# A two-layer network on one core: the second layer's tiles set between the last steps of the first layer

## The chip, the cores and the metric

The kernel runs on one core of a Trainium2 chip. The metric is device time in microseconds (us) for one execution, lower is better; the median of three runs is given.

## The reference

The input is x of 8 batches of 512 tokens of width 256, and a condition of 64 numbers for each batch. Everything is float32 at the interface. Two layers follow one another.

```
layer 0:  h  = gamma * x * rsqrt(mean(x*x) + eps) + beta            (gamma, beta from the condition)
          x  = x + alpha * W_o(softmax(q k^T / 4) v)                (16 heads of 16)
          h  = the same norm with its own gamma and beta
          x2 = x + alpha' * (out_w(silu(gate_w h) * (hidden_w h)) + out_b)      (1024 hidden)
layer 1:  h  = x2 * scale * rsqrt(mean(x2*x2) + eps)                (scale from the condition)
          val, gate = up_w h                                        (1024 each)
          h  = val * gelu(gate)                                     (exact gelu)
          y  = quantised(h, 127 levels a token) @ ternary(down_w)^T
          out = y + x2
```

## The kernel before

**First layer.** `STEPS` is 32. A batch takes up to three times 32 steps, and three batches are in work at once: iteration i prepares batch i+1 (norm, projections), runs the scores and weights of batch i, and does the output projection and the feed-forward part of batch i-1. Iterations go from -1 to 8. Every engine has its own instruction stream, written out by the same walk over iterations and steps z (`run_pipeline`, `timeline`); a step's time T says in which iteration and step it falls (T modulo 32 is z). Engines meet only by semaphores; `need` writes such a wait. Each engine takes its stream strictly in order.

For the last batch (number 7) the scores' row maxima (`maxima`, L693) run to iteration 7, z=17, the scores, exponentials and weighted sums to z=28 and 30; `heads_out` (L708) is at z=0 of iteration 8, `turn_o` at z=1, `project_o` at z=4 and 5, the residual, squares, `xnorm`, turning (`norm_t`), `affine`, and the split into a high part on ScalarE and a low part on GpSimd by z=11. The feed-forward part has 16 chunks (`T_GH`, z=14 to 28, two of them in z=19): `gate_hidden` makes 12 products into bank gen[n % 2], ScalarE takes the tanh, VectorE two operations (`swiglu`, L740), ScalarE and GpSimd split the result (`a_high`, `a_low`), and `swiglu_down` makes 6 products two steps later. Two chunks are under way at once. Products are made in three passes of high and low parts (`exact`, L895). In iteration 8 all of this has no other batch beside it.

**Ternary weights.** In iteration 8, z=4, VectorE sums the absolute values of down_w, scales, rounds (L758 to L773), with a small product and 16 turnings on TensorE; the raw weights are loaded once the last scores are made, into the space of the stacked queries and keys (qst, kst), and the result goes where the values were (vst).

**Second layer.** Only when both halves of x2 of the last batch are made, TensorE turns the 32 blocks of up_w (`transpose_weights`, eight groups of four; ScalarE and VectorE split them), into the space of the gate weights. Then 32 tiles of 128 tokens, in a software pipeline of its own (`iteration_b`, a step a tile). In step k: VectorE `scale_b` of tile k+1 (L829), `norm_b` of k+2, `h_mul(0)` of k, `finish` of k-2, `h_mul(1)`, `q_copy` (L859) of k-1, `quantise` (L842 to L854) of k; TensorE `unit(0)` of k (12 products with 512 columns), `down` of k-2 (L1152), `unit(1)` of k, `q_transpose` of k-1 (L1145), `norm_t_b` of k+2; ScalarE the high part of h for k+1 (L625), square of k+3 (L629), gelu for both halves (L634); GpSimd the root, the low part and the rounding (`integers`). The turned x2 has its bank in gen[0] (`xt_bank`), the down product in gen[1] (`down_bank`).

Names and lines that come up: DVE = VectorE, ACT = ScalarE, POOL = GpSimd, SP = the queue that issues DMAs. L693 row maxima, L895 all three-pass products, L974 weighted sums, L1010 turn_o, L722/L727 low parts of o, L738 residual, L669 xnorm, L679 affine, L743/L747 swiglu, L552 a_high, L661 low parts of turned weights, L761 to L773 ternary weights.

## Time and profile before

| | us |
|---|---|
| median of 3 runs | 1233.23 |
| lowest, highest | 1226.01, 1234.82 |
| the profiled execution, its own time | 1228.62 |
| its span, first to last instruction | 1226.8 |

Times in the trace count from the start of the span. The span and the time lie 1.8 us apart, so a difference in the one is a difference in the other. TensorE's clock is shown as the share of full speed that was granted, between two levels, 1.2 and 2.4 GHz.

### The profile page before, as it was taken

The page shows a single profiled execution, that of the slowest core. Times are in us where ns is not written, and L with a number is a line of the kernel's source. Part 1 is how long each engine was busy: PE and PEld are TensorE (multiplying, and loading weights), DVE is VectorE, ACT ScalarE, POOL GpSimd, SP SyncE. Part 2 cuts the span into 40 slices and gives each one's busy share as a digit, 9 for nine tenths or more (in the row PEclk, how much of TensorE's full clock was granted, in tenths as well). Part 3 has the DMA queues.
Part 4 walks back from the last instruction along what each step waited for, and adds up shares of the span by engine and source line. Part 5 has one row for each costly group of instructions (what it writes and reads, how often), then busy time and mean ns, then how long its engine had stood idle before and what let it go on. Part 6 is the DMA issues. An engine that isn't in the chain of part 4 may idle for free.

```text
span 1226.8 us, 19035 instructions
## 1 busy us (share of the span) xinstructions
PE 1077.7 (88%) x6775; PEld 739.2 (60%) x6775; DVE 812.8 (66%) x1613; ACT 557.8 (45%) x1242; POOL 300.3 (24%) x372
## 2 busy tenths in 40 slices
PE   6467787998989899899989989988976989999997
PEld 4312324675577467557646746753856867777775
DVE  4165556667756866775786677676443468888886
ACT  3215445655645654574566557455532332322321
POOL 0401101321321232132123213211213233333331
PEclk8757878999999999999999999998987889999999
DMA  5362624606152360634426065250040011121111
GB/s 171 77 114 51 138 49 88 128 30 135 58 100 38 98 141 17 135 75 83 64 98 131 5 132 100 58 118 2 2 150 1 28 38 53 53 63 54 53 59 36
DMA packets 87758, 92.69 MB, mean 76 GB/s; under 512 B 10241, under 2 KB 85001, under 8 KB 86641
## 3 DMA queue, kind: packets, MB, share of 16 engines
q1 hardware_dynamic: 87664, 91.49, 33.3%
q8 instruction: 54, 0.88, 0.3%
q14 instruction: 40, 0.32, 0.1%
HBM read 61.68 MB, written 29.78 MB: 75 GB/s over the span
## 4 chain that ended last, share of the span: by engine, by line
PE 71%; DVE 10%; DMA 6%; issue 4%; SPq 3%; POOL 3%; ACT 3%; POOLq 0%; DVEq 0%; ACTq 0%
PE gen L895 27%; PE core L895 13%; PE pvb L974 9%; PE core L948 7%; PE core L962 7%; DVE negmax L693 4%; DMA xa<-in_x_dram 3%; SPq L310 2%; PE gen L1152 2%; ACT xn L522 1%; DVE xn L669 1%; PE gen L935 1%; POOL stat L430 1%; PE pvb L1145 1%; DMA v_d<-v 1%
## 5 line engine op out<-in xcount | busy, mean ns | idle before, releaser
L693 DVE TENSOR_REDUCE negmax<-core 128x1 f32<-128x512 f32 x512 | 338.6, 685 | 216.8 <-PE core L948 214.6
L534 ACT ACTIVATE p<-core 128x512 f32<-128x512 f32 x512 | 278.2, 597 | 189.7 <-PE core L962 187.3
L948 PE MATMUL core<-kst,qst 96*128 96x512 bf16 x512 | 202.5, 413 | 60.4 <-DVE negmax L693 26.5
L895 PE MATMUL gen<-hs,wgh 128*128 128x256 f32 x1536 | 221.2, 295 | 9.1 <-DVE a L747 5.8
L895 PEld LDWEIGHTS gen<-hs,wgh 128*128 128x128 f32 x1536 | 198.4, 192 | 28.0 <-DVE a L747 9.0
L895 PE MATMUL core<-wgh,hs 128*128 128x512 f32 x768 | 193.8, 402 | 1.8 <-POOL hs L490 1.8
L450 POOL TENSOR_TENSOR a<-a 128x256 fp32r<-128x256 f32 x128 | 93.6, 731 | 333.0 <-ACT a L552 333.0
L962 PE MATMUL core<-qst,kst 99*128 99x512 bf16 x512 | 163.8, 400 | 8.0 <-ACT p L534 4.9
L895 PEld LDWEIGHTS core<-wgh,hs 128*128 128x128 f32 x768 | 140.8, 190 | 30.5 <-POOL hs L490 2.4
L948 PEld LDWEIGHTS core<-kst,qst 96*128 96x128 bf16 x512 | 47.1, 99 | 184.6 <-DVE negmax L693 80.5
L974 PE MATMUL pvb<-p,vst 128*32 128x512 f32 x1024 | 129.0, 623 | 0.0
L895 PE MATMUL gen<-wout,a 128*128 128x256 f32 x768 | 113.0, 285 | 1.1 <-POOL a L450 1.1
L552 ACT CAST a<-a 128x256 fp32r<-128x256 f32 x128 | 52.0, 406 | 111.9 <-DVE a L747 86.1
L895 PEld LDWEIGHTS gen<-wout,a 128*128 128x128 f32 x768 | 100.2, 190 | 3.5 <-ACT a L552 1.3
L625 ACT CAST hs<-h 128x256 fp32r<-128x256 f32 x32 | 13.0, 407 | 155.4 <-DVE h L834 155.4
L743 DVE SCALAR_TENSOR_TENSOR ug<-th,gen 128x256 f32<-128x256 f32 x128 | 52.8, 412 | 39.6 <-ACT th L547 39.6
L962 PEld LDWEIGHTS core<-qst,kst 99*128 99x128 bf16 x512 | 51.2, 102 | 46.0 <-ACT p L534 14.1
L840 DVE TENSOR_TENSOR qst<-core,p 128x512 f32<-128x512 f32 x64 | 44.2, 692 | 40.2 <-PE core L895 22.9
L974 PEld LDWEIGHTS pvb<-p,vst 128*32 128x32 f32 x1024 | 27.5, 112 | 70.2 <-issue 66.8
L496 POOL TENSOR_SCALAR kst<-qst 128x1024 bf16<-128x1024 f32 x32 | 33.4, 1044 | 143.4 <-DVE qst L854 143.4
L547 ACT ACTIVATE th<-gen 128x256 f32<-128x256 f32 x128 | 48.8, 381 | 42.0 <-PE gen L895 39.3
L428 POOL TENSOR_SCALAR stat<-stat 128x4 f32<-128x4 f32 x16 | 3.1, 193 | 257.9 <-ACT xn L522 257.9
(137 smaller groups left out, 1284.2 us busy)
## 6 DMA issues: line engine op xcount, KB each, us to landing
parts_d<-qk SPq DMA_DIRECT2D x32, 384.0 KB, 2.6
qst<-parts_d SPq DMA_DIRECT2D x96, 128.0 KB, 4.7
kst<-parts_d SPq DMA_DIRECT2D x96, 128.0 KB, 7.8
v_d<-v SPq DMA_DIRECT2D x8, 1024.0 KB, 11.2
vst<-v_d SPq DMA_DIRECT2D x16, 512.0 KB, 6.0
xa<-in_x_dram SPq DMA_DIRECT2D x8, 512.0 KB, 9.4
xr<-in_x_dram SPq DMA_DIRECT2D x8, 512.0 KB, 8.8
x_d<-x SPq DMA_DIRECT2D x8, 512.0 KB, 7.3
```

The costliest lines, as they stand in the source:

```text
L450: pool.tensor_tensor(a2[1][:, n % 2, :], a32[:, n % 2, :], a2[0][:, n % 2, :].bitcast(F32), ALU.subtract).then_inc(s["a_lo"], 1)
L496: pool.tensor_scalar(qi[t % 2], q32[t % 2], -ROUND, 1.0, ALU.add, ALU.mult).then_inc(s["qi_"], 1)
L534: act.activation(p32[:, ring(b, m), k * S:(k + 1) * S], stb[k], ACT.Exp, scale=SCALE).then_inc(s["exp_"], 1)
L547: act.activation(th[:, n % 2, :], gen[n % 2][:, 0:HALF], ACT.Tanh, scale=0.5).then_inc(s["tanh_"], 1)
L552: act.copy(a2[0][:, n % 2, :], a32[:, n % 2, :]).then_inc(s["ah"], 1)
L693: dve.tensor_reduce(negmax[:, n // TT, n % TT:n % TT + 1], smb[n % 2], AX_X, ALU.max, negate=True).then_inc(s["smax"], 1)
L743: dve.scalar_tensor_tensor(out=ug[:, n % 2, :], in0=th[:, n % 2, :], scalar=1.0, in1=gen[n % 2][:, 0:HALF], op0=ALU.add, op1=ALU.mult).the ...
L840: dve.tensor_tensor(hb[t % 2][:, c * S:(c + 1) * S], stb[c], ge[:, c, 0:S], ALU.mult).then_inc(s["hmul"], 1)
L895: last = pe.matmul(out_, l, r, start=start and i == 0, stop=stop and i == len(passes) - 1, **kw)
L948: pe.matmul(smb[n % 2], qst[0:KROWS, h, q * P:(q + 1) * P], kst[0:KROWS, h, :], start=True, stop=True).then_inc(s["smax_mm"], 1)
L962: last = pe.matmul(stb[k], kst[0:KROWS + NPART, h, kt * P:(kt + 1) * P], qst[0:KROWS + NPART, h, :], start=True, stop=True)
L974: last = pe.matmul(pvb[j * VW:(j + 1) * VW, :], vst[:, kt, GROUP * g + j, :], p32[:, ring(b, m - 1 + j // 2), (j % 2) * S:(j % 2 + 1) * S] ...
```

## The change

The tiles of the second layer are written into the same walk as the steps of the first. From iteration 7, z=30 on (`Z_TILES`), every step holds half of a tile's step: even ones `first_half` (scale_b, norm_b, unit(0), h_mul(0), down, finish, the squares and the low part), odd ones `second_half` (unit(1), q_transpose, norm_t_b, h_mul(1), q_copy, quantise, integers). So `unit` of tile 0 is at z=4 and 5 of iteration 8, and that of tile 13 at z=30 and 31; tiles 14 to 31 follow in `run_after`. Further:

- The ternary weights are made at z=10 to 13 of iteration 7, one part a step, with their two turnings of eight blocks in bank gen[1].
- The up weights are turned at z=29, 30, 31 of iteration 7 and z=0 of iteration 8, two groups a step, in the four banks of the scores.
- For the last batch all chunks use bank gen[0] (so gate_hidden n waits for the swiglu of n-1), and chunk operations of VectorE, ScalarE and GpSimd stand in the same step as the products, after the other work and ahead of the half tile. o and its projection use gen[0] and gen[2].
- gen[1] is both the bank of the turned x2 and, in its other half, that of the down product. `down` waits in addition until the tile three further on is scaled, `norm_t_b` until the tile four before is finished.
- Buffers move so that nothing of the last batch is overwritten.

```diff
-    Z_TERN = 4
+    Z_TERN = 10
+    Z_UP = 29
+    Z_TILES = 30
+    T_SLOTS = 2
...
-        wup = wgh
+        wdown = sb("wdown", [P, KF, D], BF16)
...
+        wup = [nc.alloc_sbuf_tensor_at(f"wup{n}", [P, KD, 2 * F], F32R, offset=stack_at + n * H * S * 2) for n in range(2)]
...
+        raw_up = [v3_flat.rearrange("p (n i) -> p n i", i=D), raw_hp[:, :].rearrange("p (n i) -> p n i", i=D)]
+        raw_down = v3_flat[:, 0:KD * F]
...
-        xt_bank = gen[0][:, 0:KD * P]
-        down_bank = gen[1][:, 0:D]
+        xt_bank = gen[1][:, 0:KD * P]
+        down_bank = gen[1][:, D:2 * D]
...
+        up_bank = smb + stb
+        tern_bank = gen[1][:, :].bitcast(BF16)
+        def two_banks(b, pair):
+            return (0, 2) if b == B - 1 else pair
+        def gh_bank(b, n):
+            return gen[0] if b == B - 1 else gen[n % 2]
...
+        FIRST_TILE = L_SQ3
+        N_BETWEEN = STEPS - Z_TILES + STEPS
+        def run_between(i, z, first_half, second_half):
+            n = z - Z_TILES if i == B - 1 else z + STEPS - Z_TILES if i == B else -1
+            if n >= 0:
+                (first_half, second_half)[n % T_SLOTS](tile_at(FIRST_TILE + n // T_SLOTS))
+        def run_after(first_half, second_half):
+            for step in range(FIRST_TILE + N_BETWEEN // T_SLOTS, B * TT + L_DOWN):
+                first_half(tile_at(step))
+                second_half(tile_at(step))
...
# SP
+                if i == B - 1:
+                    sp.wait_ge(s["v_st"], 16 * B)
+                    sp.dma_start(raw_down.rearrange("p (r i) -> p r i", i=F), w["down_w"].rearrange("(r p) i -> p r i", p=P)).then_inc(s["raw_down_load"], 16)
...
+                if i == B - 1:
+                    sp.wait_ge(s["tern_t_"], 2)
+                    for n in range(2):
+                        sp.dma_start(raw_up[n], w["up_w"][n * F:(n + 1) * F, :].rearrange("(r p) i -> p r i", p=P)).then_inc(s["raw_up_load"], 16)
+                for z in range(STEPS):
+                    run_between(i, z, first_half, second_half)
...
# ScalarE
+                    for n, t in enumerate(T_GH):
+                        for b in at(z, t):
+                            if b == B - 1:
+                                tanh(b, n)
+                                a_high(b, n)
+                    for n in range(len(WG_UP) // 2):
+                        if i * STEPS + z == (B - 1) * STEPS + Z_UP + n:
+                            split_up(n)
+                    run_between(i, z, first_half, second_half)
...
# VectorE
+                    if i == B - 1 and 0 <= z - Z_TERN < 4:
+                        ternary_weights(z - Z_TERN)
+                    for n, t in enumerate(T_GH):
+                        for b in at(z, t):
+                            if b == B - 1:
+                                swiglu(b, n)
...
+            def first_half(at):
+                for b, t in at(L_H3):
+                    scale_b(b, t)
+                for b, t in at(L_XN3):
+                    norm_b(b, t)
+                for b, t in at(0):
+                    h_mul(b, t, 0)
+                for b, t in at(L_DOWN):
+                    finish(b, t)
+            def second_half(at):
+                for b, t in at(0):
+                    h_mul(b, t, 1)
+                for b, t in at(L_QT):
+                    q_copy(b, t)
+                for b, t in at(0):
+                    quantise(b, t)
...
# TensorE
-                need(pe, "a_", NCH, b, n - 1)
+                need(pe, "a_", NCH, b, n if b == B - 1 else n - 1)
...
+            def ternary_weights(step):
+                if step == 0:
+                    pe.wait_ge(s["xt_"], 2 * (B - 1))
+                    pe.wait_ge(s["wsum"], 1)
+                    pe.matmul(gen[1][:, 0:1], ones[:, :], wabs[:, :], start=True, stop=True).then_inc(s["wsum_mm"], 1)
+                if step >= 2:
+                    n = step - 2
+                    pe.wait_ge(s["tern"], 1)
+                    if n == 1:
+                        pe.wait_ge(s["tern_c"], 1)
...
+                need(pe, "final", TT, b, t - L_DOWN + L_XT3 + 1)
...
                 need(pe, "q_tc", TT, b, t + 1)
                 need(pe, "final", TT, b, t)
+                pe.wait_ge(s["h32_3"], KD * min(b * TT + t + L_DOWN - L_H3 + 1, B * TT))
                 for j in range(KF):
                     last = pe.matmul(down_bank, qT[t % 2][:, j * P:(j + 1) * P], wdown[:, j, :], start=(j == 0), stop=(j == KF - 1))
...
+            run_pipeline(pe, iteration)
+            run_after(first_half, second_half)
```

## Rows read from the trace of the kernel before

**Rows 1.** The page: busy time of each engine; the chain that ended last.
```profile
PE 1077.7 (88%) x6775; PEld 739.2 (60%) x6775; DVE 812.8 (66%) x1613; ACT 557.8 (45%) x1242; POOL 300.3 (24%) x372
...
PE 71%; DVE 10%; DMA 6%; issue 4%; SPq 3%; POOL 3%; ACT 3%; POOLq 0%; DVEq 0%; ACTq 0%
```
**Rows 2.** Windows: PE, PEld, DVE, ACT, POOL busy; clock; DMA share; GB/s.
```profile
902.30:937.30 35.00, 16.27 (x109) 13.19 (x107) 17.35 (x27) 6.70 (x18) 5.17 (x6) 0.71 0.38 132
937.30:974.70 37.40, 35.97 (x288) 35.28 (x288) 14.76 (x34) 12.15 (x32) 14.09 (x17) 0.95 0.00 1
974.70:989.00 14.30, 7.78 (x38) 6.82 (x37) 9.45 (x18) 7.02 (x18) 3.10 (x7) 0.64 0.36 110
989.00:1215.50 226.50, 226.19 (x1308) 179.34 (x1308) 183.06 (x375) 59.79 (x151) 75.77 (x120) 0.99 0.17 51
1215.50:1226.80 11.30, 4.33 (x33) 2.67 (x32) 5.17 (x10) 0.00 (x0) 1.04 (x1) 0.75 0.08 28
```
**Rows 3.** Timeline of one steady tile: start, duration, engine, line, operation.
```profile
1038.04 0.62 PE L1145 MATMUL pvb<-ident_bf,kst 128*128 128x128 bf16 x8
1038.30 0.69 DVE L840 TENSOR_TENSOR qst<-core,p 128x512 f32<-128x512 f32 x1 [0.44 <-PE core L895]
...
1041.26 0.75 DVE L854 TENSOR_SCALAR qst<-qst,qs 128x1024 f32<-128x1024 f32 x1
...
1041.49 1.05 PE L1152 MATMUL gen<-vst,kst 128*128 128x256 bf16 x8
1041.92 0.60 DVE L834 TENSOR_SCALAR h<-gen,cur 128x128 f32<-128x128 f32 x2
...
1045.14 0.62 PE L1145 MATMUL pvb<-ident_bf,kst 128*128 128x128 bf16 x8
```
**Rows 4.** Timeline of the ternary weights, VectorE.
```profile
913.50 2.28 DVE L761 TENSOR_REDUCE wabs<-kst 128x1 f32<-128x2048 f32 x1
...
919.43 1.23 DVE L771 TENSOR_SCALAR kst<-kst 128x2048 bf16<-128x2048 f32 x1
...
922.64 1.22 DVE L773 COPY vst<-core 128x2048 bf16<-128x2048 bf16 x1 [1.98 <-PE core L1058]
```
**Rows 5.** Timeline in iteration 7, about z=11: VectorE's row maxima.
```profile
849.74 3.10 DVE L693 TENSOR_REDUCE negmax<-core 128x1 f32<-128x512 f32 x5
```
**Rows 6.** Timeline of the last batch's own chain and of the turned weights.
```profile
910.32 1.91 PE L1010 MATMUL gen<-ident,o 128*128 128x128 f32 x8 [1.68 <-DVE o L717]
...
912.09 1.49 DVE L727 TENSOR_TENSOR hs<-gen,hs 128x512 fp32r<-128x512 f32 x2 [1.82 <-ACT hs L572]
...
925.65 0.69 DVE L738 TENSOR_TENSOR x<-th,xr 128x512 f32<-128x512 f32 x1
...
930.83 1.14 DVE L669 TENSOR_SCALAR xn<-x,stat 128x256 f32<-128x256 f32 x4 [3.07 <-POOL stat L430]
...
933.25 1.59 DVE L679 TENSOR_SCALAR h<-gen,cur 128x512 f32<-128x512 f32 x2 [1.28 <-PE gen L935]
...
978.86 0.69 DVE L661 TENSOR_TENSOR wgh<-gen,wgh 128x512 fp32r<-128x512 f32 x1 [0.16 <-ACT wgh L516]
```
**Rows 7.** The chain that ended last, in order of time: a chunk; the squares.
```profile
876.57 2.13 PE gen L895 x18
...
927.71 1.71 ACT xn L522 x8
```
**Rows 8.** Timeline of a chunk of the last batch: tanh, first swiglu operation, cast.
```profile
966.94 0.38 ACT L547 ACTIVATE th<-gen 128x256 f32<-128x256 f32 x1 [0.35 <-PE gen L895]
...
967.36 0.42 DVE L743 SCALAR_TENSOR_TENSOR ug<-th,gen 128x256 f32<-128x256 f32 x1 [1.21 <-ACT th L547]
...
968.26 0.41 ACT L552 CAST a<-a 128x256 fp32r<-128x256 f32 x1 [0.94 <-DVE a L747]
```
**Rows 9.** Groups by line, ScalarE, 1020 to 1200 us: gelu.
```profile
L634 ACT ACTIVATE p<-core 128x512 f32<-128x512 f32 x51 | 30.0, 588 | 2.5
```
**Rows 10.** Timeline: ScalarE ahead of the first gelu.
```profile
989.01 1.28 ACT L634 ACT_TABLE_LOAD   x1
```

More of the change, by code:

```diff
@@ L546, in tanh @@
                 need(act, "u_", NCH, b, n - 1)
-                act.activation(th[:, n % 2, :], gen[n % 2][:, 0:HALF], ACT.Tanh, scale=0.5).then_inc(s["tanh_"], 1)
+                act.activation(th[:, n % 2, :], gh_bank(b, n)[:, 0:HALF], ACT.Tanh, scale=0.5).then_inc(s["tanh_"], 1)
             def a_high(b, n):
@@ L571, in o_high @@
                     need(act, "o_t", KD, b, k + 1)
[L572 removed]
+                    act.copy(hs[0][:, k, :], gen[two_banks(b, OT_BANK)[k]][:, :]).then_inc(s["oh"], 1)
             def iteration(i, *there):
@@ new lines, in iteration, with split_up, first_half @@
+                    run_between(i, z, first_half, second_half)
+            def split_up(n):
+                for g in (2 * n, 2 * n + 1):
+                    act.wait_ge(s["up_t"], g + 1)
+                    act.copy(WG_UP[g][1][0], up_bank[g % 4]).then_inc(s["up_hi"], 1)
+            def first_half(at):
+                for b, t in at(L_HH3):
+                    if b == 0 and t == 0:
+                        act.wait_ge(s["up_t"], len(WG_UP))
+                    need(act, "h32_3", KD * TT, b, KD * (t + 1))
+                    need(act, "v2_mm", 2 * TT, b, 2 * (t + 1 - TT))
+                    a = slice(t * P, (t + 1) * P)
+                    act.copy(hp[0][:, :, a], h32_b[:, :, a]).then_inc(s["hh3"], 1)
+                for b, t in at(L_SQ3):
+                    if b == 0 and t == 0:
+                        act.wait_ge(s["pv_mm"], NG * KT * B)
+                    need(act, f"x2_ld{t}", 16, b, 16)
+                    need(act, "xt3", TT, b, t + 1 - TT)
+                    act.activation(xn_b[:, t, :], xa[:, t, :], ACT.Square, accum_out=stat[:, 1, 0, t:t + 1]).then_inc(s["sq3"], 1)
+                for b, t in at(0):
+                    gelu(b, t, 0)
@@ L639, in _, with second_half, gelu @@
+            def second_half(at):
+                for b, t in at(0):
+                    gelu(b, t, 1)
+            def gelu(b, t, c):
+                need(act, "g_mm", 2 * TT, b, 2 * t + c + 1)
+                need(act, "hmul", 2 * TT, b, 2 * t + c - 1)
+                act.activation(ge[:, c, :], smb[c], ACT.Gelu).then_inc(s["gelu"], 1)
+            run_pipeline(act, iteration)
+            run_after(first_half, second_half)
         @block.vector
@@ L816, in iteration @@
                             qk_rest(b, j)
-            run_pipeline(dve, iteration)
-            split_lo(WG_UP, "up_hi", "up_lo")
+                    if i == B - 1 and 0 <= z - Z_TERN < 4:
+                        ternary_weights(z - Z_TERN)
+                    for n, t in enumerate(T_GH):
+                        for b in at(z, t):
+                            if b == B - 1:
+                                swiglu(b, n)
+                    for n in range(len(WG_UP) // 2):
+                        if i * STEPS + z == (B - 1) * STEPS + Z_UP + n:
+                            split_up(n)
+                    run_between(i, z, first_half, second_half)
             def norm_b(b, t):
@@ L1115, in iteration @@
                             turn_group(b, m // (2 * KT))
-            run_pipeline(pe, iteration)
-            pe.wait_ge(s["x2_"], 2 * B)
-            pe.wait_ge(s["raw_up_load"], 16)
-            transpose_weights(WG_UP, "up_t", "up_lo")
-            pe.wait_ge(s["up_lo"], len(WG_UP))
-            pe.wait_ge(s["tern_c"], 1)
+                    if i == B - 1 and 0 <= z - Z_TERN < 4:
+                        ternary_weights(z - Z_TERN)
+                    for n in range(len(WG_UP) // 2):
+                        if i * STEPS + z == (B - 1) * STEPS + Z_UP + n:
+                            turn_up(n)
+                    run_between(i, z, first_half, second_half)
             def norm_t_b(b, t):
@@ L1138, in unit @@
                     need(pe, free, 2 * TT, b, 2 * t + c - 1)
-                    exact(bank, [(col(hs, k, t * P, P), col(wup, k, first + c * S, S)) for k in range(KD)]).then_inc(s[sem_], 1)
+                    exact(bank, [(col(hp, k, t * P, P), col(wup, k, first + c * S, S)) for k in range(KD)]).then_inc(s[sem_], 1)
             def q_transpose(b, t):
+                if b == 0 and t == 0:
+                    pe.wait_ge(s["o_norm"], NG * B)
                 need(pe, "qi_", TT, b, t + 1)
```

277 lines of the change are left out of this document (133 added, 144 removed).

## The prediction

> **What bounds the kernel now.** I read the page's engine table and its chain of waits first: TensorE is busy for 88% of the span and carries 71% of the chain that ended last [rows 1]. An average over stages does not say what filling one stage is worth, so I cut the last third into stretches [rows 2]. The reader should see two full stretches and three holes. From 902.3 us (last score of the last batch) to 937.3 (its first feed-forward chunk) TensorE is busy for 16.3 of 35.0 us at a mean granted clock of 0.71; that is the one-off chain of turning, projecting, residual, norm and affine. The 16 chunks to 974.7 are nearly full. From 974.7 to 989.0, where the up weights are turned, 7.8 of 14.3 us. Then 32 tiles of the second layer in 226.5 us, full. The last 11.3 us drain. So the holes hold 18.7 + 1.4 + 6.5 + 7.0 us, and the last can't be filled. Next I looked at one steady tile in the timeline [rows 3]: TensorE goes 1038.04 to 1045.14, so 7.10 us a tile without a gap; within it, 3.45 us from the quantised turning to the down product (turnings and a half of the unit) and 3.65 us for the down product and the other half.
>
> **The tile alone: a new wait.** down() now waits for h32_3 of the tile three further on, since both use bank gen[1]. That is scale_b (L834) of the same step, the first thing VectorE does in first_half, but it comes after the whole of quantise. In rows 3 VectorE's h_mul starts at 1038.30, quantise's last operation at 1041.26 and the scaling at 1041.92 for 0.60 us, so until 1042.52; TensorE started the down product at 1041.49. Nothing in the diff moves VectorE's queue, which starts anew from the end of TensorE's half (0.26 us after 1038.04). So the down product starts at about 1042.57, 1.08 us late. Queued behind it on TensorE are the second half of the unit, the quantised turning and norm_t, and for that half wait ScalarE's gelu and VectorE's h_mul, whose end starts the next round. The period becomes 4.53 + 3.65 = 8.18 us. Fourteen tiles now lie between, 18 remain, 17 of them wait (the last has no later tile to wait for): 17 x 8.18 + 7.10 = 146.2 us. Bounds: no wait at all (127.8), if VectorE ran earlier, which nothing in the diff does, or twice the wait (164.6), if the granted clock falls in the gaps. I take the rows' value.
>
> **Ternary weights, moved into steps 10 to 13 of iteration 7.** Before they ran in the tail, from 913.50 until the copy at 922.64 is over (923.9), all on VectorE or waiting for it [rows 4]. Now their 2.28 us reduction, 4.1 us of scaling (920.66 less 915.78, less 0.8 for the handing over to TensorE and back) and two half copies of about 0.7 us stand in steps where VectorE already limits the scores: it runs five row maxima in a row there, with TensorE waiting [rows 5], and TensorE waits in order for wsum, tern and tern_c, with the next scores, and so ScalarE's exponentials, behind it. Stepping through the queues I get 3.3 us after step 11, 7.2 after step 13. Bounds: 0 (the idle time around takes it all) and 10.4 (the whole of rows 4). I take 7.2. The loads of the raw weights find empty DMA queues; their waits are met long before on SP, and I cost them at nothing.
>
> **Weights turned and the heads' last turning.** The turnings (32) now stand in steps 29 to 32 between others; per group of four, VectorE's low part is 0.69 us [rows 6]. ScalarE's copies and VectorE's subtractions come ahead of o_out and heads_out on their queues, and I get turn_o at 913.7 in place of 910.3: +3.4 us (bounds 0 and 5.5, eight subtractions).
>
> **From turn_o to the first chunk.** Before: 27.0 us. Now 3.3 us until the low part of o (910.32 to 913.58, rows 6), then project_o (2.84) and five tiles without their first two down products and the first quantised turnings: about 34.6 us of TensorE work with norm_t (ten halves of a unit at 2.77, which is 3.65 less 0.88 for a down product; three down products; 0.68 for the turnings of a tile, 3.45 less 2.77; 0.9 for norm_t). Into VectorE's and ScalarE's queues come the residuals (0.69 each instruction), xnorm (1.14), affine (1.59) [rows 6] and squares (1.71) [rows 7] of the last batch, each before a scale_b for which TensorE now waits. In step 8 the squares have held back gelu and h_mul, xnorm follows, and the down product waits 6.6 us; in step 10 the affine makes it 2.6; in step 12 the 1.1 of the bare tile. Sum 3.3 + 2.84 + 34.6 + 10.3 = 51.0 us. Bounds of the waits: 0, and 14 (the residuals in full too).
>
> **The chunks.** A chunk costs TensorE 2.13 us (18 products, rows 7). With a single bank a gate_hidden waits for the swiglu before it: tanh 0.38, then 0.42 + 0.42 on VectorE, plus the handing over, some 1.7 us [rows 8]; the half tile between two chunks (3.45 or 3.65) hides it, except in step 19, which has two chunks. A pair of steps is 2 x 2.13 + 7.10 = 11.36 us. VectorE needs 3.62 us after h_mul, 0.87 for swiglu and 0.60 to scale, and so is just ready when TensorE comes to the down product: cover without reserve. Sum to step 31: 16 x 2.13 + 9 tiles x 7.10 + waits (1.7; 0.6 at the first; 1.2 and 0.5 at the residuals) = 102 us. Bounds of the waits: 1.7, and 9 x 1.08 + 1.7 if the cover is gone.
>
> **The sum,** against the profiled execution (span 1226.8, time 1228.6): 910.3 + 7.2 + 3.4 + 51.0 + 102.0 + 146.2 + 11.3 (drain, unchanged) = 1231.4, and 1.6 for half-clock starts behind the new gaps (the clock mean of 0.71 in 35 us shows that such gaps cost): 1233.0, 6.2 us more than before. Said otherwise, the holes give back some 32 us; 18.4 go into the new wait, 7.2 into iteration 7, 14.3 into new waits between. The profiled execution lies 4.6 us below the median of 1233.2, so I forecast 1233.2 + 6.2, or 1239 us. Its own range is 1228 to 1248. About 1% (12 us) is what a measurement of this kernel can tell from no change.
>
> **Rivals.** *Table loads, slower.* Chunks use Tanh, tiles Gelu, now in turn on ScalarE. The trace has one ACT_TABLE_LOAD between them, 1.28 us, as the first gelu comes [rows 10]; exponentials, tanh, squares and casts share what was loaded before, squares and casts also what comes after. Whether tanh and gelu can share one, no row shows. If not, there are some 30 loads in steps 14 to 28, four a pair, three of them on the round from h_mul to h_mul: 3.62 (quantise) + 0.87 (swiglu) + 0.60 (scale) + 0.46 (cast) + 0.43 (square, a quarter of 1.71) + 1.28 + 0.59 (gelu) [rows 9] + 1.28 + 0.38 (tanh) + 0.87 + 0.46 (cast) + 1.28 + 0.59 and 0.2 of handing over = 12.9 us, against 11.36 of TensorE. That decides from the point where the round exceeds TensorE's pair: 1.54 x 7.5 = 11.6 us more, 1251 us. Against it: tanh already shares with exp, so it is no function that needs a set of its own. The Trainium skill, "ScalarE: Activation LUTs", "Table sets: the hidden batching unit", says that activations should be batched by set, and lists tanh beside exp and beside sigmoid but not beside gelu; the trace's single load agrees as far as it goes. The same page, "What ACT_TABLE_LOAD costs", puts a switch at 2.66 us with a drain of 1.38; by an estimate with that figure the round would be 17 us and the kernel some 1282 us; no row here shows the drain.
>
> *The cover holds, faster.* If the idle time in iteration 7 takes the ternary work (0 for 7.2) and VectorE's in-order queue holds nobody up in steps 8 to 13 and 14 to 31 (0 for 14.3), 21.5 us come off: 1218 us. It decides where scale_b ends before TensorE has ended the half of its step. For it: VectorE is busy for only 17.35 of 35.0 us before the chunks [rows 2]; against it: a bare tile already misses by 1.08 us.
>
> *The tiles don't move.* If SP's loads of x2 stood behind a late wait, the 14 tiles would come after and cost 8.18 in place of 7.10 (32 x 1.08 = 35 us in all, 16 more than forecast), the chunks would have no cover (16 x 1.7 = 27 us), and of the 32 us of holes only the 14.3 of the turned weights would come back (18 less): some 1300 us. But SP's last wait ahead of the tiles that stand in iteration 8, x2 of batch 6, is met at about step 31, so I give this next to nothing.
>
> **How the numbers follow.** My forecast 0.45, table loads 0.38, cover holds 0.13, others 0.04. Faster by over 1% (under 1221): most of the third, 0.10. Slower by over 1% (over 1245.5): two thirds of the table case, the heavier cases, a little of the first, 0.08: 0.40. Within 1%: 0.50. The range takes in the table case at its rows' price and the edge of the fast one: 1216 to 1265.
>
> **What would show it.** Right: a period of 8.2 us in the last 18 tiles with about 1.1 us of idle TensorE ahead of each down product, released by VectorE's L834 counterpart; ternary reduction near 850 us with TensorE waiting for VectorE, and the last scores some 7 us late; first chunk at about 972 us; pairs of about 11.4 us in the chunks. ACT_TABLE_LOAD count 2 for my forecast, about 30 for the first rival, with pairs of 12.9 us. Wrong: a period of 7.1 us in the last tiles, which would take 18 us off the sum, or gaps of many microseconds elsewhere.

## The result, and the profile after

| | before | after |
|---|---|---|
| median, lowest to highest (us) | 1231.23, 1226.01 to 1234.82 (4 runs) | 1254.89, 1251.70 to 1257.61 (4 runs) |
| the profiled execution, its span (us) | 1228.62, 1226.8 | 1251.70, 1249.9 |
| ratio after to before | | 1.0195, 95% interval 1.0146 to 1.0243 |

The kernel became about 2% slower, 24 us. The page of the kernel after (busy time; the chain that ended last), beside [rows 1]:

```profile
PE 1074.5 (86%) x6775; PEld 736.5 (59%) x6775; DVE 812.2 (65%) x1614; ACT 556.9 (45%) x1242; POOL 302.3 (24%) x372
...
PE 63%; DVE 16%; DMA 7%; issue 6%; SPq 3%; ACT 3%; POOL 2%; POOLq 0%; DVEq 0%; ACTq 0%
```

No engine's busy time has changed by more than 3.2 us. TensorE's share of the chain fell from 71% to 63% and VectorE's rose from 10% to 16%: the same work waits more for VectorE. Windows of the kernel after (length; PE, PEld, DVE, ACT, POOL busy; clock; DMA share; GB/s), beside [rows 2]:

```profile
836.00:867.00 31.00, 19.41 (x86) 7.67 (x86) 23.20 (x37) 10.10 (x24) 4.70 (x4) 0.61 0.00 1
...
1080.40:1238.50 158.10, 140.44 (x814) 109.77 (x813) 113.20 (x232) 35.19 (x89) 44.95 (x70) 1.00 0.17 50
```

The first is the ternary weights' stretch in iteration 7: TensorE idle for 11.6 of 31 us, at a mean clock of 0.61. The second holds the last tiles: 17.7 of 158.1 us idle where [rows 2] had 0.3 of 226.5, and at full clock. The sum can be set against the prediction's at landmarks in the timeline: the issue of SP's last shift stores (`shift`: the softmax shifts are written to memory and loaded back for the scores, qst<-shift_d), `turn_o`, the first chunk, the last unit. Times in us; "predicted" is the term of the prediction, for an addition to before or for a stretch:

| stretch | predicted | after |
|---|---|---|
| start to the shift store three before the last (800.40 before) | +0 | 795.77, -4.6 |
| from there to the last shift store (68.4 before) | +7.2 | 83.5, +15.1 |
| from there to turn_o (41.5 before) | +3.4 | 46.5, +5.0 |
| turn_o to the first chunk | 51.0 | 59.3 (925.75 to 985.02) |
| chunks, to the end of step 31 | 102.0 | 107.1 (to 1092.1) |
| 18 last tiles | 146.2 | 146.4 (to 1238.5) |
| drain; half-clock starts | 11.3; 1.6 | 11.4; the starts lie inside the stretches above |
| end | 1233.0 | 1249.9 |

The first stretch is code that the change doesn't touch, and in the profiles of this study it ended anywhere from 795.8 to 806.0 us. To compare profiles I therefore use the rest: **span less the start of that shift store**. It is 1226.8 - 800.4 = 426.4 us before and 454.1 after, so 27.7 more. It varies too, from one profile each: two kernels below that differ in nothing that was found to matter have 454.1 and 451.1.

**The last tiles.** Timeline of the kernel after, one steady tile, beside [rows 3] (start, duration, engine, line, operation, idle time before and who ended it):

```profile
1116.04 0.62 PE L1250 MATMUL pvb<-ident_bf,v 128*128 128x128 bf16 x8
1116.30 0.69 DVE L927 TENSOR_TENSOR p<-core,p 128x512 f32<-128x512 f32 x1 [1.58 <-PE core L983]
...
1119.92 0.60 DVE L921 TENSOR_SCALAR qk<-gen,cur 128x128 f32<-128x128 f32 x2
...
1120.67 1.03 PE L1258 MATMUL gen<-wdown,v 128*128 128x256 bf16 x8 [1.02 <-DVE qk L921]
```

From the quantised turning to the down product: 4.63 us, where [rows 3] have 3.45. TensorE idles 1.02 us, and the releaser is L921, `scale_b`. The chain puts the down products at 1112.41, 1120.67 and 1128.94: a period of 8.27 us, not 7.10.

**Iteration 7.** Timeline of the kernel after, in place of [rows 4]:

```profile
849.29 2.28 DVE L832 TENSOR_REDUCE wabs<-v 128x1 f32<-128x2048 f32 x1
...
853.19 1.08 ACT L583 ACTIVATE p<-core 128x512 f32<-128x512 f32 x2 [8.85 <-PE core L1050]
...
854.86 3.47 POOL L477 TENSOR_TENSOR hs<-h,hs 128x512 fp32r<-128x512 f32 x2 [15.48 <-ACT hs L576]
855.04 2.17 DVE L839 TENSOR_SCALAR v<-v,winv 128x2048 f32<-128x2048 f32 x1
...
857.24 2.17 DVE L841 TENSOR_SCALAR v<-v 128x2048 f32<-128x2048 f32 x1
...
862.65 1.09 ACT L583 ACTIVATE p<-core 128x512 f32<-128x512 f32 x2 [6.37 <-PE core L1050]
```

ScalarE's exponentials, one of the two engines that the scores keep going, stand still for 8.85 and 6.37 us. The two scaling operations take 2.17 us each beside a GpSimd operation that itself takes 3.47 us. And earlier, when SP has issued the 1 MB load of down_w, the small shift store lands late. SP's queue and the scores that wait, kernel after:

```profile
808.83 0.43 SPq L379 DMA_DIRECT2D v<-in_L_cond_down_w_dram  x1
...
817.94 0.77 SPq L359 DMA_DIRECT2D shift_d<-shift  x1
...
825.87 0.26 SPq L362 DMA_DIRECT2D qst<-shift_d  x1
827.55 0.61 PE L1050 MATMUL core<-qst,kst 99*128 99x512 bf16 x2 [2.35 <-DMA qst<-shift_d]
```

The same two issues in the kernel before:

```profile
822.57 0.32 SPq L324 DMA_DIRECT2D shift_d<-shift  x1
...
826.55 0.26 SPq L327 DMA_DIRECT2D qst<-shift_d  x1
```

SP issues the load back once the store has landed: 7.9 us after it, before 4.0.

**No table loads.** Groups by line, ScalarE, whole kernel after, and the timeline ahead of the first gelu, beside [rows 9, 10]:

```profile
L565 ACT ACT_TABLE_LOAD x1 | 1.3, 1283 | 0.7 <-PEq L1291 0.7
L703 ACT ACT_TABLE_LOAD x1 | 1.3, 1283 | 0.0
```
```profile
1008.35 0.38 ACT L596 ACTIVATE th<-gen 128x256 f32<-128x256 f32 x1 [2.83 <-PE gen L983]
...
1012.12 0.58 ACT L703 ACTIVATE p<-core 128x512 f32<-128x512 f32 x1
...
1014.08 0.38 ACT L596 ACTIVATE th<-gen 128x256 f32<-128x256 f32 x1 [1.38 <-PE gen L983]
```

Two loads in all, as before. Tanh (L596) and gelu (L703) alternate without one. The measured time lies near the first rival's 1251 us, but by coincidence: its mechanism did not occur.

### The profile page after: what moved, and what is told of

Same layout as the page of the kernel before. It is cut to its first block, busy times and chain, and to the rows that moved or that the text cites. A ratio compares the mean times of both kernels' runs of the same rounds, so it can differ in the third digit from the quotient of the medians.

```text
span 1249.9 us, 19053 instructions
## 1 busy us (share of the span) xinstructions
PE 1074.5 (86%) x6775; PEld 736.5 (59%) x6775; DVE 812.2 (65%) x1614; ACT 556.9 (45%) x1242; POOL 302.3 (24%) x372
## 4 chain that ended last, share of the span: by engine, by line
PE 63%; DVE 16%; DMA 7%; issue 6%; SPq 3%; ACT 3%; POOL 2%; POOLq 0%; DVEq 0%; ACTq 0%
PE gen L983 26%; PE core L983 8%; PE pvb L1062 8%; PE core L1036 7%; PE core L1050 6%; DVE negmax L763 4%; DMA xa<-in_x_dram 3%; SPq L345 2%; PE gen L1258 2%; DVE qs L933 2%; ACT xn L571 1%; DVE xn L739 1%; DMA shift_d<-shift 1%; PE gen L1023 1%; DVE qk L921 1%
## 5 line engine op out<-in xcount | busy, mean ns | idle before, releaser
L1036 PE MATMUL core<-kst,qst 96*128 96x512 bf16 x512 | 203.4, 414 | 58.8 <-DVE negmax L763 24.2
L983 PE MATMUL core<-wup,hp 128*128 128x512 f32 x768 | 191.5, 398 | 1.7 <-POOL hp L536 1.7
L983 PEld LDWEIGHTS core<-wup,hp 128*128 128x128 f32 x768 | 140.7, 190 | 29.8 <-POOL hp L536 2.0
L1062 PE MATMUL pvb<-p,vst 128*32 128x512 f32 x1024 | 125.7, 609 | 0.0
L927 DVE TENSOR_TENSOR p<-core,p 128x512 f32<-128x512 f32 x64 | 44.3, 692 | 90.5 <-PE core L983 57.7
L1050 PEld LDWEIGHTS core<-qst,kst 99*128 99x128 bf16 x512 | 51.2, 102 | 48.1 <-ACT p L583 13.0
L596 ACT ACTIVATE th<-gen 128x256 f32<-128x256 f32 x128 | 49.0, 382 | 60.1 <-PE gen L983 58.7
L544 POOL TENSOR_SCALAR v<-p 128x1024 bf16<-128x1024 f32 x32 | 33.6, 1050 | 171.4 <-DVE p L941 171.4
L686 ACT CAST hp<-qk 128x256 fp32r<-128x256 f32 x32 | 13.0, 405 | 118.9 <-DVE qk L921 118.1
L1258 PE MATMUL gen<-wdown,v 128*128 128x256 bf16 x256 | 35.7, 286 | 31.8 <-DVE qk L921 30.0
```

Of the source, the lines that this page charges most:

```text
L596: act.activation(th[:, n % 2, :], gh_bank(b, n)[:, 0:HALF], ACT.Tanh, scale=0.5).then_inc(s["tanh_"], 1)
L927: dve.tensor_tensor(hb[t % 2][:, c * S:(c + 1) * S], stb[c], ge[:, c, :], ALU.mult).then_inc(s["hmul"], 1)
L983: last = pe.matmul(out_, l, r, start=start and i == 0, stop=stop and i == len(passes) - 1, **kw)
L1036: pe.matmul(smb[n % 2], qst[0:KROWS, h, q * P:(q + 1) * P], kst[0:KROWS, h, :], start=True, stop=True).then_inc(s["smax_mm"], 1)
L1050: last = pe.matmul(stb[k], kst[0:KROWS + NPART, h, kt * P:(kt + 1) * P], qst[0:KROWS + NPART, h, :], start=True, stop=True)
L1062: last = pe.matmul(pvb[j * VW:(j + 1) * VW, :], vst[:, kt, GROUP * g + j, :], p32[:, ring(b, m - 1 + j // 2), (j % 2) * S:(j % 2 + 1) * S] ...
```

## The experiments

Each run of a kernel had runs of the kernel before beside it, on the same chip. Ratios are to those, with their 95% interval; "rest" is span less the start of that shift store, from one profile each.

### The shared bank: undone, and put alone into the kernel before

The turned x2 of tiles from 16 on goes to gen[0], which the chunks have left by then; nothing else moves.

```diff
+        FIRST_LATE = 16
+        def xt_of(b, t):
+            return gen[0][:, 0:KD * P] if b * TT + t >= FIRST_LATE else xt_bank
...
-                need(pe, "final", TT, b, t - L_DOWN + L_XT3 + 1)
+                if b * TT + t < FIRST_LATE:
+                    need(pe, "final", TT, b, t - L_DOWN + L_XT3 + 1)
+                if b * TT + t == FIRST_LATE:
+                    pe.wait_ge(s["a_"], NCH * B)
...
-                pe.wait_ge(s["h32_3"], KD * min(b * TT + t + L_DOWN - L_H3 + 1, B * TT))
+                pe.wait_ge(s["h32_3"], KD * min(b * TT + t + L_DOWN - L_H3 + 1, FIRST_LATE))
```

> The changed kernel, but from tile 16 on the turned x2 has bank gen[0], which the chunks have left, so the down products of steps 15 and later wait no longer for scale_b. Theory (the shared bank costs each of the last tiles 1.16 us, 8.27 less 7.11): the period of those tiles is 7.1 us again and 16 x 1.16 = 18.5 us come off, span about 1231. Rival (the other new places, rounding and quantised values in v3 and p32, or the new order of the queues, hold the tiles up): the period stays at 8.0 us or more and less than 3 us come off.

Measured: 1233.66 us (10 runs) beside 1228.60 (13 runs), ratio 1.0057 (1.0025 to 1.0088). Rest 435.2, 18.9 less than after (18.5 of it from the last chunk's down products to the last unit). The chain of waits of this kernel (start, duration, what):

```profile
1129.64 2.77 PE core L988 x12
1132.40 0.89 PE gen L1266 x8
1133.29 2.76 PE core L988 x12
1136.06 0.46 PE pvb L1258 x8
1136.52 0.23 PE gen L1239 x2
1136.75 2.76 PE core L988 x12
```

Only TensorE, from one half unit at 1129.64 to its successor at 1136.75: 7.11 us. So the wait is the bank's. The other way round, the wait alone goes into the kernel before:

```diff
                 need(pe, "final", TT, b, t)
+                pe.wait_ge(s["h32_3"], KD * min(b * TT + t + L_DOWN - L_H3 + 1, B * TT))
```

> The kernel before with one line more: down waits until the tile three further on is scaled, as in the changed kernel; the banks stay apart, so the wait protects nothing there. Theory: all but the last tiles wait, period 8.2 to 8.3 us, 29 x 1.16 = 34 us more than before, ratio about 1.027. Rival (the wait is met early, and what costs is where the buffers lie): under 3 us more.

Measured: 1261.04 us, ratio 1.0240 (1.0165 to 1.0315); 1.027 was expected, inside the interval. Rest 463.5, 37.1 more than before. The chain in this kernel's tiles:

```profile
1111.38 1.03 PE gen L1153 x8
...
1119.64 1.03 PE gen L1153 x8
```

The period is 8.26 us (8.28 to the next, at 1127.92) with no bank moved. The price holds from both sides: some 1.16 us for each tile that has no chunk beside it. One line of waiting, alone, makes this kernel 2.4% slower.

### The load of down_w behind the shift

SP issues the load after the second shift of the scores instead of ahead of it.

```diff
-                if i == B - 1:
-                    sp.wait_ge(s["v_st"], 16 * B)
-                    sp.dma_start(raw_down...)
...
                     shift(i, 1)
+                if i == B - 1:
+                    sp.wait_ge(s["v_st"], 16 * B)
+                    sp.dma_start(raw_down...)
```

> The changed kernel, but the 1 MB load of down_w is issued after the second shift of iteration 7 instead of ahead of it. Theory (the shift's store stood behind the load for 7.9 us and held up the scores): the store takes 2 us or less there and 4 us come off, 0.3%. Rival (the store is slow for its own 12 KB scattered writes, or the scores wait on something else): under 1 us.

Measured: 1253.32 us, ratio 1.0196 (1.0133 to 1.0260). The time can't tell it from after; the profile can. SP's queue in this kernel:

```profile
819.80 0.32 SPq L359 DMA_DIRECT2D shift_d<-shift  x1
823.42 0.26 SPq L362 DMA_DIRECT2D qst<-shift_d  x1
```

The store lands in 3.6 us (2 or less was expected), and from this shift store to the next it is 22.0 us, after 26.1; the rest is 450.0, 4.1 less too. That is the far end of the price. In the eight profiled kernels of this study with the load ahead the store took 5.3 to 8.2 us to land, in the four with it behind 3.6 to 5.2. The two stretches from the landmark to the shift store that is at 844.01 after took 45.1 to 48.2 us with the load ahead (seven kernels, without `Z_TERN = 9`), 44.2 to 45.5 with it behind (three) and 44.2 before: 1.6 us between the means.

### Why the scaling took 2.17 us an operation

Three kernels. First, is it that the operation reads and writes the same buffer?

```diff
-dve.tensor_scalar(raw_down, raw_down, winv[:, 0:1], 1.0, ALU.mult, ALU.min)
+dve.tensor_scalar(raw_hp[:, 0:KD * F], raw_down, winv[:, 0:1], 1.0, ALU.mult, ALU.min)
...
-dve.tensor_scalar(raw_down, raw_down, -1.0, ROUND, ALU.max, ALU.add)
+dve.tensor_scalar(raw_down, raw_hp[:, 0:KD * F], -1.0, ROUND, ALU.max, ALU.add)
```

> The changed kernel, but the first two scaling operations of the ternary weights go from one buffer to another and back, as before, instead of in place. Theory (in place, a tensor_scalar of 2048 runs at half speed, 2.17 us): both take 1.2 to 1.3 us, 1.8 us come off, 0.15%. Rival (GpSimd's low part of h beside it slows VectorE): the first, beside it, stays near 2.2 us, and at most one gets faster.

Measured: 1251.36 us, ratio 1.0184 (1.0121 to 1.0246). Timeline:

```profile
858.59 3.47 POOL L477 TENSOR_TENSOR hs<-h,hs 128x512 fp32r<-128x512 f32 x2 [13.55 <-ACT hs L576]
858.76 2.17 DVE L839 TENSOR_SCALAR raw_hp<-v,winv 128x2048 f32<-128x2048 f32 x1
860.97 2.17 DVE L841 TENSOR_SCALAR v<-raw_hp 128x2048 f32<-128x2048 f32 x1
```

Still 2.17 us twice, with GpSimd's L477 beside it again, so it is not that the operation works in place. The rest is 451.1, 3.0 less than after, although the scaling is as slow: so much do profiles differ without the edit. Then a step earlier, to take it away from GpSimd's work.

```diff
-    Z_TERN = 10
+    Z_TERN = 9
```

> The changed kernel with Z_TERN 9: the ternary weights stand one step earlier, so the scaling is at step 10, where GpSimd has nothing to do. Theory (VectorE's tensor_scalar falls to half speed while GpSimd's low part of h runs beside it): the two slow operations take 1.25 us instead of 2.17 and 1.8 us come off. Rival (something about the buffers' place makes them slow): both stay at 2.17.

Measured: 1255.96 us, ratio 1.0225 (1.0185 to 1.0265), operations of 2.38 and 2.17 us. GpSimd's L477 started at 856.01 and lay beside them once more, so this run separated nothing. So a step later instead, with the wait for the bank that this step needs:

```diff
-    Z_TERN = 10
+    Z_TERN = 11
...
+                if b == B - 2 and n == 1:
+                    pe.wait_ge(s["tern_c"], 2)
```

> The changed kernel with Z_TERN 11: the scaling is at step 12, after GpSimd's low part of h (step 11). Theory (VectorE's tensor_scalar runs at half speed beside a GpSimd operation on the same memory): L839 and L841 take 1.25 us instead of 2.17, and GpSimd's two subtractions 2.5 us instead of 3.47. Rival (the place of the buffers makes them slow): 2.17 again. The whole gains 2 us at most.

Measured: 1253.53 us, ratio 1.0199 (1.0149 to 1.0249). Timeline:

```profile
849.57 2.49 POOL L477 TENSOR_TENSOR hs<-h,hs 128x512 fp32r<-128x512 f32 x2 [9.72 <-ACT hs L576]
...
850.35 2.27 DVE L832 TENSOR_REDUCE wabs<-v 128x1 f32<-128x2048 f32 x1
...
856.08 1.29 DVE L839 TENSOR_SCALAR v<-v,winv 128x2048 f32<-128x2048 f32 x1
857.40 1.23 DVE L841 TENSOR_SCALAR v<-v 128x2048 f32<-128x2048 f32 x1
```

Apart, VectorE needs 1.29 and 1.23 us and GpSimd 2.49. Added up that is 5.01 us; together, in the kernel after, the same four instructions took from 854.86 to 859.41, 4.55 us. So they gained little by running beside each other, 0.46 us of 5.01; the long durations can be read as taking turns. Not every VectorE operation does: the reduction L832 lies beside L477 here and takes 2.27 us, where in the kernel after, with no GpSimd operation beside it, it took 2.28. The Trainium skill, "SBUF — State Buffer", "SBUF: two separate sides", describes an exclusive lock on a port pair that VectorE and GpSimd share, held for a whole instruction, with the other engine blocked; it says this of VectorE operations in a two-port performance mode or with two inputs in SBUF. No row here shows an operation's mode; the durations of the two scaling operations agree with such a lock. The rest is 451.0, 3.1 less than after, but that is no more than the 3.0 above, where the scaling stayed slow: the 1.8 us are seen in the two operations and not in the whole.

### x2 of the first batch loaded ahead

In the kernel after, `turn_o` ends at 926.8 but ScalarE takes its result only after a square that waits for x2 of tile 1. Timeline of the kernel after:

```profile
925.35 1.41 SPq L434 DMA_DIRECT2D xa<-x_d  x3
925.75 1.09 PE L1098 MATMUL gen<-ident,o 128*128 128x128 f32 x8 [1.31 <-DVE o L787]
...
930.58 0.42 ACT L692 ACTIVATE p<-xa 128x256 f32<-128x256 f32 x1 [5.36 <-DMA xa<-x_d]
...
931.00 1.05 ACT L621 CAST hs<-gen 128x512 fp32r<-128x512 f32 x2
```

The load is issued only at 925.35, on a queue where it stands behind the stores of batch 6. The edit lets SP issue the four loads of batch 0 with that of its first tile:

```diff
+                    if b == 0 and t > 0:
+                        continue
                     need_sp("xn3", TT, b, t + 1 - TT)
-                    sp.dma_start(xa[:, t, :], tile_of(x2_d, b, t)).then_inc(s[f"x2_ld{t}"], 16)
+                    for t in range(TT) if b == 0 else (t,):
+                        sp.dma_start(xa[:, t, :], tile_of(x2_d, b, t)).then_inc(s[f"x2_ld{t}"], 16)
```

> The changed kernel, but SP issues the loads of x2 for tiles 1 to 3 with that of tile 0, in iteration 7, instead of in steps 32, 34 and 36, where they stand behind the wait for x2 of batch 6 and its store. Theory (ScalarE, waiting in order for tile 1, holds o_high of the last batch up): ScalarE's wait of 5.4 us for xa goes, and turn_o to the first projection shrinks by 4 to 5 us. Rival (the chain waits on VectorE there anyway): under 1.5 us.

Measured: 1250.26 us, ratio 1.0172 (1.0133 to 1.0211). turn_o to the first chunk 54.8 us in place of 59.3: 4.5 less. In the other profiles with all fourteen tiles between it is 59.1 to 61.2 us with the loads as after, and 54.3 and 56.5 in the two combined kernels below, which have them ahead. (The rest, 444.5, is 9.6 less; 4.9 of that lies in iteration 7, which the edit doesn't touch, and is the varying price of the down_w load at least in part.)

### What five tiles beside the last batch's chain are worth

The tiles begin at about the first chunk, so none stands between the heads, projection and norm of the last batch; the five follow at the end.

```diff
-    Z_TILES = 30
+    Z_TILES = 40
```

> The changed kernel with Z_TILES 40: the tiles begin with the unit of tile 0 in step 14 of iteration 8, beside the first chunk; nothing of a tile but its norm stands in steps 1 to 13, and nine tiles lie between instead of fourteen. Theory (in steps 1 to 13 tiles and the last batch's chain hold each other up on the in-order queues): turn_o to the first chunk falls from 65.1 to about 30 us, the chunks stay near 101 us, and five more tiles at 8.27 follow: 41.4 less 35, so some 6 us slower than the changed kernel; the five tiles were worth only that. Rival (those steps are well filled): turn_o to the chunk stays above 40 and it is 15 us slower or more.

Measured: 1256.96 us, ratio 1.0236 (1.0190 to 1.0282). turn_o to the first chunk 20.4 us, 38.9 less than after (the 65.1 of the expectation is not the 59.3 of this landmark); from the last chunk's down products to the end of the last unit 196.3, 41.0 more, where five tiles at 8.27 are 41.4. The rest is the same, 454.1, and the median 2.1 us above that of after, inside the intervals, where 6 was expected. The chain of this kernel without tiles, timeline:

```profile
931.17 5.49 PE L983 MATMUL gen<-wo,hs 128*128 128x256 f32 x24 [1.62 <-DVE hs L797]
...
942.46 1.97 PE L1023 MATMUL gen<-ident,xn 128*128 128x128 f32 x8 [5.80 <-DVE xn L739]
```

and in the kernel after, with tiles, at the same norm:

```profile
956.90 1.92 DVE L739 TENSOR_SCALAR xn<-x,stat 128x256 f32<-128x256 f32 x4
958.73 0.60 DVE L921 TENSOR_SCALAR qk<-gen,cur 128x128 f32<-128x128 f32 x2
...
959.48 1.86 PE L1258 MATMUL gen<-wdown,v 128*128 128x256 bf16 x8 [4.19 <-DVE qk L921]
```

Five tiles beside the chain stretch it by 38.9 us, 7.8 each, though TensorE was idle for more than half of it before. The norm waits on VectorE behind a tile's quantise, then the tile's down product waits 4.19 us behind the norm; each chain holds up the other. Some 4.5 of the 38.9 us are the x2 loads of the run before.

### Ternary weights where VectorE has room

Steps 20 to 23 of iteration 7 instead of 10 to 13: the row maxima are over by z=17. Their turnings and sum use the first bank of the maxima.

```diff
-    Z_TERN = 10
+    Z_TERN = 20
-        tern_bank = gen[1][:, :].bitcast(BF16)
+        tern_bank = smb[0].bitcast(BF16)
...
-                    pe.wait_ge(s["xt_"], 2 * (B - 1))
+                    pe.wait_ge(s["smax"], 2 * STEPS * B)
...
                     pe.wait_ge(s["raw_up_load"], 16 * 2)
+                    pe.wait_ge(s["tern_c"], 2)
```

> The changed kernel with nothing changed but the ternary weights, in steps 20 to 23 and bank smb[0]. Theory (they cost 11 us at steps 10 to 13, 2 us here): 9 us off the changed kernel, ratio to before about 1.011. Rival (the 11 us come from the load of down_w and the shift, which stay): 2 us off at most.

Measured: 1247.78 us, ratio 1.0131 (1.0072 to 1.0190). The stretch of iteration 7 is 69.6 us in place of 83.5 (and of 78.6 to 82.9 in the four other kernels that have the load and the ternary weights placed as after); the one after it, where the weights now stand, is 48.1 in place of 46.5; the rest 443.7, 10.4 less than after. (The down_w load is still ahead of the shift here, and its price varies; the sum of the two is what the combined kernel below shows.)

### All together

Bank, down_w load, `Z_TERN = 9` and x2 loads of the above in one:

> The changed kernel with four edits: bank gen[0] for the turned x2 after the last chunk, the load of down_w behind the second shift, the loads of tiles 1 to 3 ahead, the ternary weights from step 9. Theory (the costs are apart from each other and add): 18.5 + 4.1 + 4.5 + 1.8 = 29 us off the changed kernel's 1250, span 1221, ratio to the kernel before about 0.995. Rival (taking one wait away brings up the next): less than 23 us off, and no version of it is below the kernel before.

Measured: 1230.78 us (10 runs) beside 1228.83 (13 runs), ratio 1.0001 (0.9974 to 1.0028). Rest 424.8, 29.3 less than after, as the parts promised (29). But the time is that of before, not the expected 0.995 of it: the repairs add up, bring the kernel back to before, and no further. With the ternary weights in steps 20 to 23 instead:

> As e8_all, but the ternary weights stand in steps 20 to 23 of iteration 7, in bank smb[0], which the row maxima have left, beside chunks of batch 6 where TensorE is full and VectorE under half busy. Theory (in steps 9 to 13 they sat on the path VectorE - scores - exponentials, later they have cover): the stretch from the second to the fourth shift store of iteration 7 plus what precedes it falls from 77.5 to about 69 us, steps 20 to 23 grow by 2 us, and the span is about 1214, ratio to the kernel before about 0.989. Rival (the work is as dear beside the chunks, since TensorE waits in order for it): within 3 us of e8_all.

Measured: 1221.98 us (12 runs) beside 1229.56 (23 runs), ratio **0.9935 (0.9909 to 0.9962)**. It beats both kernels, by somewhat over half of what was expected (0.989). Rest 419.4; iteration 7's stretch is 68.1 us, where before has 68.4. The 7.0 us less than before lie behind `turn_o`: from there to the end of the last unit it is 291.8 us in place of 305.4, 13.6 less, about the 14.3 us in which before turned its up weights alone; 6.5 us of that are given back ahead of `turn_o` (48.1 in place of 41.5), where the up and ternary weights now are. Its scaling operations in the timeline, and the window around them:

```profile
884.34 1.29 DVE L850 TENSOR_SCALAR v<-v,winv 128x2048 f32<-128x2048 f32 x1
885.66 1.23 DVE L852 TENSOR_SCALAR v<-v 128x2048 f32<-128x2048 f32 x1
```
```profile
872.00:920.00 48.00, 45.16 (x370) 36.28 (x362) 26.11 (x49) 25.81 (x60) 13.18 (x16) 1.00 0.20 64
```

TensorE is busy for 94% of the 48 us around the ternary weights: there the ternary weights cost 1.6 us (this stretch is 48.1 us, and 46.5 in the combined kernel that has them at step 9), and not the 9 to 11 of steps 10 to 13 (from the shift store at 844.01 to the next, 33.2 to 35.3 us in place of 24.2 before). Last, the same with `Z_TILES = 40`, to ask once more for the worth of the five tiles now that a tile at the end costs 7.1 us and not 8.27:

> As e9_tern_late, but tiles begin in step 14 of iteration 8 (Z_TILES 40), nine of them between. Theory (with the bank apart a later tile costs 7.1 us, and five tiles in steps 4 to 13 stretch the last batch's chain by 34 us, from 20.4): equal within 2 us to e9_tern_late, so tiles beside the chain gain nothing and the chunks' stretch neither; what was gained is the ternary work and the turned weights. Rival (they fill idle time): e12 is 5 us slower or more.

Measured: 1220.58 us (12 runs), ratio 0.9933 (0.9904 to 0.9963); rest 420.1. Equal to the last kernel: 37.0 us less from turn_o to the first chunk, 35.5 more at the end, 2.4 more in the chunks. Filling this hole with tiles is worth nothing, in either form.

## Why the prediction was right or wrong

The range of 1216 to 1265 us held the median of 1254.89; my likeliest case didn't. It said no change (1239, its own range to 1248) and the kernel is 2% slower, the direction that I had given 0.40, and mostly for table loads that never came. The range reached so far up for their sake, so that it held the result was in part luck. Point by point:

- **The shared bank: right, in place, mechanism and size.** 17 waits of 1.08 us were forecast, period 8.18; 8.27 was seen, 146.4 us in place of 146.2, and undoing it gave 18.9 us where the term is 17 x 1.08 = 18.4.
- **"I cost them at nothing" (the loads of raw weights): the step that failed in kind.** I looked at whether SP's waits were met and whether the queues were empty when the load starts, and not at what is issued behind it. The shift store behind the megabyte took 7.9 us to land in place of 4.0, and the scores wait for it: 4.1 us with this placement undone, 1.6 in the mean of the profiles.
- **7.2 us for the ternary work in iteration 7: mechanism right, size off.** The stretch grew by 15.1 (by 10.2 to 14.5 in the four other kernels with the same placement). With 4.1 for the load, 11.0 remain, above even the 10.4 that I had set as the bound ("the whole of rows 4"). 1.8 is the scaling at 2.17 us, which I had priced from a stretch where GpSimd was idle. The remaining 2.0 us were not tried by themselves. TensorE's clock is the nearest candidate: from the shift store at 844.01 to that at 879.27 TensorE was busy for 25.4 us at a mean granted clock of 0.74, where before, between the same two stores and with 18 products less, it was busy for 21.9 us at 0.91. That the placement is the cause is shown: ten steps later this whole stretch costs what it did before (68.1 us with the load moved too), and the next one 1.6 us more.
- **"The turned weights +3.4":** 5.0, inside its bounds.
- **51.0 us from turn_o to the first chunk: mis-sized, 59.3.** The waits of 10.3 us were right in place and nearly in size: 1.73 us ahead of a half unit and 4.19, 2.49 and 1.03 ahead of the down products, 9.4 together, where I had 6.6, 2.6 and 1.1. Two other terms were too small. I had 3.3 us from `turn_o` to the projection's products; it was 8.3 (925.75 to 934.06), and 3.7 with the x2 loads ahead (927.60 to 931.30): again a load taken as free, x2 behind batch 6's stores. And the 2.84 + 34.6 us of TensorE's own work took 41.5 (59.3 less 8.3 less 9.4), 4.1 more, 3.1 of them in the three places named below, at a lower clock. Windows of the kernel after:

```profile
934.10:936.80 2.70, 2.70 (x15) 2.70 (x14) 1.43 (x3) 1.90 (x6) 2.16 (x6) 0.50 0.17 49
959.50:961.10 1.60, 1.60 (x8) 1.14 (x9) 0.70 (x3) 1.16 (x4) 0.76 (x3) 0.50 0.05 10
```

  Behind idle time of 5.99 and 4.19 us TensorE is at the lower of its two levels. Half of the projection took 2.91 us in the first window, where the other half, after it, took 1.58; the down product in the second took 1.86 us where the one at 972.54, at a clock of 1.00, took 1.03; and the half unit at 962.70 took 3.94 us where the one at 967.08 took 2.98. The sum had 1.6 us for all such starts.
- **102 us of chunks: 107.1.** The pairs' cover was called "without reserve", and it has none. Timeline of the kernel after, two instructions that begin together, and the same VectorE operation when GpSimd is free:

```profile
1000.79 0.34 DVE L911 TENSOR_SCALAR p<-xa,stat 128x256 f32<-128x256 f32 x1
...
1011.16 2.38 POOL L487 TENSOR_TENSOR x<-x,al 128x1024 f32<-128x1024 f32 x1
1011.28 2.41 DVE L911 TENSOR_SCALAR p<-xa,stat 128x256 f32<-128x256 f32 x1
...
1029.62 1.86 PE L1258 MATMUL gen<-wdown,v 128*128 128x256 bf16 x8 [3.48 <-DVE qk L921]
```

  The bias (L487) blocks the norm for 2 us, and a down product waits 3.48 us at a place where I had none. TensorE was idle for 7.0 of the 107.1 us, within the bounds that I had given (9 x 1.08 + 1.7 = 11.4 against the 4.0 used); its own work took 100.1 us, 2.1 more than the 98.0 of the sum, at a mean clock of 0.98.
- **"The holes give back some 32 us": wrong for the hole that mattered.** Five tiles beside the chain cost 38.9 us of it, more than the 35.5 they cost at the end at 7.1 us each. In the sum I had 51.0 us with tiles; without them, the runs show that the chain takes 20.4. I had added 24 us to the old 27.0 for 35.5 us of tiles. The old 27.0 had VectorE's ternary work in it; that this work's leaving makes the 6.6 us between 27.0 and 20.4 is argued, not tried by itself.
- **Start and half-clock starts:** the untouched first stretch was 4.6 us shorter in this profile, which hid part of the misses; against the medians it is no gain. So the profile missed by 16.9 us and the median by 15.9, but from the landmark on it is 27.7 us more in place of 6.2, a miss of 21.5. The 1.6 us for half-clock starts were mis-sized: at least 3.1 in the stretch from turn_o to the first chunk alone.
- **Rivals.** Table loads: excluded by two loads in the whole trace. Cover holds: excluded as made, but with the bank, loads and ternary weights placed otherwise the kernel reaches 1221.98, near the 1218 that it named. Tiles don't move: excluded, `unit` of tile 0 starts at 936.76.

The loss is thus made of four things that moving the tiles didn't need, each read from one profile with a few microseconds of spread: 18.9 us for a bank, 4.1 and 4.5 for two loads, and 10.4 for VectorE work in a stretch that VectorE limits. One by one they come to 37.9 us, undone together to 34.7 (454.1 less 419.4): more than the 27.7 that were lost, so that the kernel without them is 7.0 us shorter in the rest than before.

## What to carry to other kernels

When a second pipeline is set into the idle time of a first, sum its instructions on every in-order queue, and not just TensorE's holes: a hole made of a dependency chain through VectorE gave nothing back, while one-off VectorE work moved to where TensorE is the bound cost 1.6 us in place of some 10. A bank shared between two stages is a wait from one to the other, and it is to be priced for each iteration (1.16 us in a 7.1 us period, on one line). Of a DMA that is moved, ask what is issued behind it, and take durations of VectorE and GpSimd only from rows where the other is as idle as it will be. A gap on TensorE can cost more than its length: behind the gaps from turn_o to the first chunk the lower clock cost 3 us more.

## What the runs showed of the hardware that I had not expected

- Some operations of VectorE and GpSimd in SBUF take turns, and the time of waiting shows as a longer duration: a 2048-wide float32 scaling 2.17 us beside GpSimd, 1.23 to 1.29 alone; a 256-wide one 2.41 us beside the bias, 0.34 alone. A reduction over 2048 values did not: 2.27 us beside GpSimd, 2.28 alone.
- TensorE's granted clock fell in the stretches with gaps, and the same products took longer there: a down product 1.86 us at 0.50, behind 4.19 us of idle time, and 1.03 at 1.00.
- The small shift store, issued 9 us after a 1 MB load with other transfers between, took 7.9 us to land in place of 4.0; over the profiles it was 5.3 to 8.2 us behind the load and 3.6 to 5.2 ahead of it.
- Tanh and gelu alternate without a table load: 16 tanh of the last batch stand among the gelus of 14 tiles, and the load count stays 2. The Trainium skill, "ScalarE: Activation LUTs", "Table sets: the hidden batching unit", lists tanh beside exp and beside sigmoid, and not beside gelu; the measurement decides.
- The same untouched code took 795.8 to 806.0 us in the profiles, a spread of 10.2 us, 0.8% of the kernel. Stretches measured from a landmark told four microseconds apart where medians of four runs didn't, but iteration 7 itself varied by as much as 5 us between profiles of the same placement, so that no single reading there is good to less.
